# Recommendation tower on one core: each tile's pair products in one burst of matmuls, or in two with a turned chunk and a lookup between

## The reference

```python
e = jnp.stack([tbl_0[ids[:, 0]], ..., tbl_25[ids[:, 25]]], axis=1)      # 2048 x 26 x 128
combined = jnp.concatenate((dense[:, None, :], e), axis=1)              # 2048 x 27 x 128
interactions = jnp.einsum('bfd,bgd->bfg', combined, combined)           # 27 x 27 a sample
z = jnp.concatenate((dense, interactions[:, iu, ju]), axis=1)           # iu < ju: 351 pairs
h = jnp.concatenate([z, dense], axis=1)                                 # 2048 x 607
h = jnp.maximum(h @ W_top1 + b_top1, 0.0)                               # 512
h = jnp.maximum(h @ W_top2 + b_top2, 0.0)                               # 256
y = h @ W_top3                                                          # 1
```

## Time and profile before

| | |
|---|---|
| median of 3 runs | 529.42 us (525.82 to 533.13) |
| profiled execution | 532.02 us |
| its span, first to last instruction | 530.2 us |
| mean granted TensorE clock | 0.865 |
| busy: TensorE, VectorE, ScalarE, GpSimd | 74%, 50%, 30%, 50% |
| DMA | 35.02 MB, 66 GB/s in the mean |

### The profile page before, as it was taken

The page is one execution under the profiler, slowest core; times in us unless marked ns, Lnnn a source line. Parts: engine busy times, 40 slices in busy tenths (PEclk is TensorE's granted clock), DMA queues, the critical chain, the costliest instruction groups (busy, mean ns, idle before and its releaser), DMA issues.

```text
span 530.2 us, 14756 instructions
## 1 busy us (share of the span) xinstructions
PE 391.2 (74%) x6474; PEld 369.2 (70%) x6474; DVE 263.0 (50%) x761; ACT 159.9 (30%) x253; POOL 264.0 (50%) x282
## 2 busy tenths in 40 slices
PE   8459557857778788688878867786876687775877
PEld 7448546757668677588768856686866686774867
DVE  5267853554535564285463835284443743445123
ACT  3235322322313233132333323042322223323232
POOL 6757474462645626365564636375462635636000
PEclk9959687979878978788988987898977979789998
DMA  9933332131221312222222312222121321201000
GB/s 196 263 99 110 97 95 57 45 70 39 56 70 45 81 33 66 52 59 82 53 66 53 80 37 60 63 65 67 45 71 39 77 54 46 74 24 40 9 3 1
DMA packets 25333, 35.02 MB, mean 66 GB/s; under 512 B 8506, under 2 KB 19154, under 8 KB 25270
## 3 DMA queue, kind: packets, MB, share of 16 engines
q0 software_dynamic: 8768, 17.97, 13.4%
q1 hardware_dynamic: 14422, 15.96, 12.3%
q10 hardware_dynamic: 2080, 0.15, 0.4%
HBM read 34.05 MB, written 0.01 MB: 64 GB/s over the span
## 4 chain that ended last, share of the span: by engine, by line
PE 52%; another core or an unknown queue 17%; issue 15%; DVE 9%; ACT 6%; POOL 0%; POOLq 0%; DVEq 0%
PE side L608 18%; PE prod L641 10%; PE mlp L661 8%; DVE onehot L487 5%; PE side L619 4%; PE side L603 4%; DVE table L501 3%; PE mlp L663 3%; ACT feats L374 2%; ACT feats L381 2%; PE mlp L680 2%; PE mlp L672 1%; ACT diag L399 1%; PE side L650 1%
## 5 line engine op out<-in xcount | busy, mean ns | idle before, releaser
L354 POOL DMA_INDIRECT rows<-in_tbl,ids x274 | 263.2, 960 | 225.0 <-PE side L619 120.9
L487 DVE TENSOR_SCALAR onehot<-wanted,row_no 125x256 fp32r<-125x256 int32 (+1 forms) x564 | 171.7, 377 | 143.9 <-remote 59.7
L608 PE MATMUL side<-onehot,table_hi 125*128 125x256 f32 x566 | 164.0, 320 | 24.4 <-issue 16.2
L608 PE MATMUL side<-onehot,table_lo 125*128 125x256 f32 x566 | 157.0, 308 | 4.0 <-issue 3.9
L608 PEld LDWEIGHTS side<-onehot,table_hi 125*128 125x128 f32 x566 | 123.7, 219 | 30.3 <-issue 22.6
L608 PEld LDWEIGHTS side<-onehot,table_lo 125*128 125x128 f32 x566 | 123.6, 218 | 5.2 <-issue 5.2
L374 ACT ACTIVATE feats<-side 128x256 f32<-128x256 f32 x71 | 47.0, 662 | 176.6 <-remote 110.0
L381 ACT ACTIVATE feats<-side 128x512 f32<-128x512 f32 (+2 forms) x80 | 78.9, 1032 | 49.4 <-remote 46.3
L641 PE MATMUL prod<-feats 128*27 128x27 f32 (+1 forms) x4096 | 52.6, 211 | 50.0 <-issue 47.2
L641 PEld LDWEIGHTS prod<-feats 128*27 128x27 f32 (+1 forms) x4096 | 47.4, 124 | 54.1 <-issue 48.4
L619 PE MATMUL side<-ident,rows 128*128 128x128 f32 x274 | 48.9, 307 | 28.0 <-ACT feats L374 20.1
(11 more groups left out here) (53 smaller groups left out, 171.1 us busy)
## 6 DMA issues: line engine op xcount, KB each, us to landing
wanted<-in_small_ids SPq DMA_DIRECT2D x63, 128.0 KB
rows<-in_tbl,ids POOLq DMA_INDIRECT x274
feats<-in_tbl SPq DMA_DIRECT2D x7, 448.0 KB
dense<-in_dense_rows SPq DMA_DIRECT2D x16, 64.0 KB
w_sb<-in_w_pairs SPq DMA_DIRECT2D x1, 702.0 KB
table<-in_tbl SPq DMA_DIRECT2D x1, 560.0 KB
w_sb<-in_tbl SPq DMA_DIRECT2D x1, 560.0 KB
w_sb<-in_w SPq DMA_DIRECT2D x1, 512.0 KB
```

Of the source, the lines that this page charges most:

```text
L354: gp.indirect_dma_start(rows[:, q % SLOTS_OF_ROWS, f * D:(f + 1) * D], None, large_tables[g + f], bass.IndirectOffsetOnAxis(ap=ids[:, t, g ...
L487: made = nc.vector.tensor_scalar(onehot[v % 2][:, c - row_nos_at(h), :], wants, row_no[:, c:c + 1], None, ALU.is_equal)
L608: last = nc.tensor.matmul(look_bank(v)[:, 0:BS], part_of(part, k)[:, c * D:(c + 1) * D], onehot[v % 2][:, c, :], start=(c == 0 and part is ...
```

## The change

A tile's products come in two parts of 64 samples each (`PARTS`), part A at the head of segment 0 and part B at the head of segment 1. Between them stand segment 0's turned chunk and lookup. Each part writes one PSUM bank, of four (`PRODS`), where before a tile wrote a buffer of two banks, of two; ScalarE reads each part as it is done. The two relu stages of the layers go from VectorE to ScalarE, with one `ACTIVATE` in place of each `TENSOR_SCALAR`; the second layer's stands in segment 1 behind the lookup, the first layer's at the end of segment 3. ScalarE's copy of the result now stands before its copy of the pairs. VectorE makes the pair table in segment 1 instead of segment 0, behind that segment's one-hots. The last tile's products were in two parts already.

```diff
-BANK_GROUPS = 16
-PART_BANKS = 2
+PARTS = 2
+PART_GROUPS = GROUPS // PARTS
+PART_COLS = PART_GROUPS * SLOTS
...
+PRODS = 4
...
-        prod = [ctx.enter_context(nc.psum_tensor(f"prod{i}", [P, PART_BANKS * BANK], F32)) for i in range(2)]
+        prod = [ctx.enter_context(nc.psum_tensor(f"prod{i}", [P, BANK], F32)) for i in range(PRODS)]
...
+            def finish_first_layer(t):
+                act.wait_ge(l1_full, t + 1)
+                for n in range(N1):
+                    last = nc.scalar.activation(h1[:, n * P:(n + 1) * P], mlp[:, n * P:(n + 1) * P], ACT.Relu,
+                                                bias=b1_sb[:, n:n + 1])
+                last.then_inc(h1_ready, 1)
...
             for t in range(LAST):
                 for s in range(SEGS):
-                    if s == 0:
-                        read_products(t)
+                    if s < PARTS:
+                        read_products(t, s)
                     for k in TURNS_AT[s]:
                         empty_turn(t + 1, k)
                     if s == 1:
                         place_dense(t + 1)
                     for v in lookups_at(t, s):
                         empty_lookup(v)
+                    if s == 1 and t >= 1:
+                        finish_second_layer(t - 1)
                     if s == PAIRS_AT:
-                        copy_pairs(t)
                         if t >= 1:
                             copy_result(t - 1)
+                        copy_pairs(t)
+                    if s == 3:
+                        if t == 0:
+                            act.wait_ge(w_in, 5 * 16)
+                        finish_first_layer(t)
...
-                    if s == 0:
-                        if t == 1:
-                            dve.wait_ge(w_in, 5 * 16)
-                        if t >= 1:
-                            finish_first_layer(t - 1)
+                    if s == 1:
                         make_table(t)
...
-                    if s == 1 and t >= 1:
-                        finish_second_layer(t - 1)
...
             for t in range(LAST):
                 for s in range(SEGS):
-                    if s == 0:
-                        products(t)
+                    if s < PARTS:
+                        products(t, s)
                     for k in TURNS_AT[s]:
                         turn_rows(t + 1, k)
```

More of the change, by code:

```diff
@@ L260, in tail_bank @@
         def tail_bank(n):
[L261 removed]
+            return prod[n][:, 0:P]
         def spread_ids(k):
[L265 removed]
+            return prod[k // 2][0:CP, k % 2 * BS:(k % 2 + 1) * BS]
         def look_bank(v):
@@ L515, in finish @@
                 return nc.vector.tensor_scalar(out[:, n * P:(n + 1) * P], bank, bias[:, n:n + 1], 0.0, ALU.add, ALU.max)
[L517 to L525, removed]
-                    last = finish(h2, mlp[:, n * P:(n + 1) * P], b2_sb, n)
-                last.then_inc(h2_ready, 1)
             def clear_pads(i):
@@ L621, in turn_rows, with products @@
                 last.then_inc(turn_full, 1)
-            def products(t, r=0):
-                m = t + r
-                if t == 2:
-                    pe.wait_ge(pads_ready, 2 * FEAT_TILES)
+            def products(t, r):
+                m = PARTS * t + r
                 if r == 0:
+                    if t == 2:
+                        pe.wait_ge(pads_ready, 2 * FEAT_TILES)
                     pe.wait_ge(side_read, SIDE_OF["turn", NC * (t + 1) - 1] + 1)
@@ L630, in products @@
                     pe.wait_ge(dense_placed, t + 1)
-                if m >= 2:
-                    pe.wait_ge(prod_read, m - 1)
-                own = W if t < 2 else SLOTS
-                for k in range(parts_of(t)[r]):
-                    for g in range(BANK_GROUPS):
-                        for i in range(GS):
-                            n = ((r + k) * BANK_GROUPS + g) * GS + i
-                            at = t % FEAT_TILES * FT + n // 2 * TWO + n % 2 * W
-                            to = k * BANK + g * SLOTS
-                            last = nc.tensor.matmul(prod[m % 2][i * W:i * W + own, to:to + SLOTS],
-                                                    feats[:, at:at + own], feats[:, at:at + SLOTS],
-                                                    start=True, stop=True, tile_position=(0, i * W))
+                if m >= PRODS:
+                    pe.wait_ge(prod_read, m - PRODS + 1)
+                own = W if m < PRODS else SLOTS
+                for g in range(PART_GROUPS):
+                    for i in range(GS):
+                        n = (r * PART_GROUPS + g) * GS + i
+                        at = t % FEAT_TILES * FT + n // 2 * TWO + n % 2 * W
+                        last = nc.tensor.matmul(prod[m % PRODS][i * W:i * W + own, g * SLOTS:(g + 1) * SLOTS],
+                                                feats[:, at:at + own], feats[:, at:at + SLOTS],
+                                                start=True, stop=True, tile_position=(0, i * W))
                 last.then_inc(prod_full, 1)
```

26 lines of the change are left out of this document (15 added, 11 removed).

## The result

| | before | after |
|---|---|---|
| median, same chip | 529.5 us (525.82 to 533.13, 4 runs) | 505.22 us (501.41 to 508.68, 4 runs) |
| ratio | | **0.954**, 95% interval 0.9425 to 0.9655 |
| profiled execution, its span | 532.02, 530.2 us | 508.68, 506.9 us |
| mean granted TensorE clock | 0.865 | 0.882 |

A forecast was written before the change was run, and what follows sets the result against it. GpSimd's gathers were taken to set the beat, 31.0 us a tile; saving 1.0 us over 14 tiles (-14 us) took the profiled 532.0 to 518, the median 2.6 lower: 516 us, own range 508 to 524, 8 in 10 493 to 535.

The forecast's parts named there:

- GpSimd's gathers give the beat, T to T: From T, the first gather after a tile's first turned chunk, to the next T: 30.0 us against 31.0.
- Part A ahead of the first chunk, -3.5 us: Before the first turned chunk: half the matmuls save 1.6 us, the code stop 1.9; bounds 1.6 and 3.7.
- the drain: Between a tile's last gather and freely running products: 1.2 us while gathers drain.
- Part B, +2.1 us: Between first and second chunk: products crawl beside gathers, delaying gather round two by 2.1 us; upper bound +3.5.
- The rest of the tile "stays": After part B: rounds of 4, 4 and 5 gathers with two waits of 1.3 us, as in tile 5.
- ScalarE's relus, nothing: Relus of layers 1 and 2 moved to ScalarE cost nothing; bound +0.7 us a tile.
- Tile 0 unchanged: At the start: tile 0, like the tail, counted as unchanged; the saving covers 14 tiles only.
- The clock covered: Second lookup: another half-clock stretch after a second crawl, 1.4 us, covered by a late signal; without cover +0.5.
- four banks nothing: Four PSUM banks instead of two pairs remove no wait, as products never waited for a read: nothing.
- B is free: Rival, 20%: gathers don't hold part B, which is hidden in tiles like 4; 28.6 us a tile, 495 us.
- Stops stay: Rival, 17%: stops come from how products run, not the packet boundary, so each burst keeps one; 530 us.
- TensorE becomes late: Rival, 11%: crawls, half-clock stretches and late signals make TensorE late, third chunk ending after T+14.1; 543 us.

The follow-up runs named there:

- B behind the chunk: Changed kernel with part B right behind the first turned chunk, ahead of segment 0's lookups: 588.2 us, ratio 1.1023.
- B behind the second chunk: Changed kernel with part B behind the second turned chunk, in segment 1, instead of ahead of it: 573.35 us, ratio 1.0771.
- the third set: Changed kernel (374.11 us, 0.884) and three variants of it rerun beside the kernel before, unchanged, which took 423.58 us here and 538.43 in the first set.
- Split alone: Changed kernel with the relus of layers 1 and 2 back on VectorE: 521.49 us, ratio 0.975; rerun later at 375.39 us, ratio 0.8885.
- relus alone: Kernel before with the relus on ScalarE and the result's copy ahead of the pairs', products in one burst: 530.48 us, ratio 0.9915.
- B ahead of the chunk: Changed kernel with part B straight behind part A, ahead of the first turned chunk, four banks and ScalarE's relus kept: 534.82 us, ratio 0.9989.
- the kernel before once more: Kernel before, unchanged, run again for its trace on a third chip: 530.96 us beside 531.13 of its twin, ratio 1.006.
- the runs without gathers: Kernels before and after, each without the gathers of tiles 3 to 15 and the waits for them: 437.54 us (ratio 0.8215) and 386.25 us (0.7245).
- the second layer ahead of B: Changed kernel with the second layer of the tile before moved ahead of part B in even tiles: 375.49 us, ratio 0.8884.

## Why the prediction was right, step by step

**GpSimd's gathers give the beat, T to T.** Right in form and nearly in size: 29.7 for 30.0. The closeness is in part luck, as two terms below are each 0.7 us off and cancel. The sum itself is loose: its path (8.1 + 4.7 + ... + 1.1) adds up to 29.9 and not 29.8, and the parts, -3.5 and +2.1, make 1.4 us a tile, where it takes 1.0. By its parts it would have said about 510 (14 times 0.4 less).

**Part A ahead of the first chunk, -3.5 us.** Measured -2.77. The stops for code are gone (13 of 14 tiles before, none of 1.5 us or more that isn't a crawl after), and the halves cost 1.1 to 1.3 us unhindered. 0.7 us were oversized, inside the bounds of 1.6 and 3.7. What is missing is mostly the drain, for which the sum had 1.2 us: in nine of tiles 2 to 13 the long piece of A starts 1.7 to 1.9 us after the last gather has ended (tile 7: 266.83 and 268.67), and in tiles 5, 6 and 12 TensorE itself gets to A only 2.4 to 3.6 us after it.

**Part B, +2.1 us.** Measured +2.11 in the mean. B ends at T+6.4 to 6.8 (forecast 7.0), round two starts at T+7.3 to 8.1, 7.7 in the mean (forecast 8.1). The mean is of two kinds: even tiles, where B crawls, have round two 2.3 to 3.1 us later than before, odd ones 1.1 to 1.6. B behind the chunk and B behind the second chunk show the mechanism from both sides: the crawl lasts while gathers do.

**The rest of the tile "stays".** It lost 0.71 us of waits. Perhaps the wait before round two spaces the gathers, so that turned chunks and free places meet more evenly; no run separates it.

**ScalarE's relus, nothing.** On their own they gave 0.85% (interval 0.34 to 1.34%), some 4.6 us, possibly by a wait the prediction had not counted, the third layer's for VectorE. On top of the split no run resolves them: 0.954 and 0.975 come from different chips and their intervals nearly meet, and in the third set the two lie 0.3% apart. Split alone and relus alone multiply to 0.967; the rest to 0.954 isn't assigned.

**Tile 0 unchanged.** This step failed. It is also split, and its part A lets the first T come 1.9 us sooner (63.48 for 65.40); and the wait before round two breaks up a row of twelve gathers beside which TensorE had stood for 7.88 us. 7.9 us by tile 2, where the sum had 3 (its 14 tiles less the 11 from there on). That it is the split's doing fits the other traces: tile 2 has its T at 124.5 with the split alone, and at 129.3, 136.8 and 134.6 with the relus alone, with B ahead of the chunk and with the kernel before once more. Of the 9.3 us between the forecast's 14 and the 23.3 of the two spans, 4.9 are this term, 2.8 the tiles and 1.6 the end.

**The clock covered, four banks nothing.** Clock: 0.882 after 0.865, no loss. Banks: b ahead of the chunk has them and gains nothing, 0.9989.

**The rivals.** *B is free* (495) is wrong at this level, since B crawls, and right at the other: there both parts take 1.3 to 2.0 us from first to last start, but for one of tiles 0 to 14 (3.5). *Stops stay* (530) is excluded by the runs without gathers, by the packets that land at the stops, and by the order of B ahead of the chunk, which brings them back and lands at 534.82. *TensorE becomes late* (543) is what B right behind the chunk (588.2) and behind the second chunk (573.35) do: each passes the point that the prediction named, a third chunk later than T+14.1 (14.8 to 18.0 and 17.9 to 18.8 in tiles 2 to 13; 11.0 to 12.7 in the changed kernel).

**What stays open.** What makes TensorE crawl and signals come late. Gathers are needed (without them neither occurs), but they are not enough (in the third set they run back to back beside full-speed products). Something must be added that differs between sets of runs on one and the same chip, and no row of the profile names it. It isn't late code: in B of tile 2 handfuls go from 125.40 to 127.92, and packets of code were fetched at 122.2 and 129.5 only. Nor are transfers slower at the slower level: in the two traces of the changed kernel a packet of code takes 1.06 and 1.05 us in the mean, a packet of the gathers 0.12 and 0.13. One rival stands untested. Handfuls of five each 0.7 us are one matmul in some 0.15 us (an estimate from the rows of B right behind the chunk), close to the 0.12 us at which lookups start anyway. A limit on how fast instructions reach TensorE beside gathers would then hold up products and leave lookups alone. The experiment that was to tell this from other readings, the second layer ahead of B, ran at the level without a crawl.

## What to carry to other kernels

A long burst of small matmuls can outrun its own code. If a timeline shows "issue" stops that stand behind the same matmul in trace after trace, put other, slower work of the same engine in the middle: here 64 calls, a chunk and a lookup of 16 or more matmuls, then the other 64, and try it with the parts adjacent as well, since that shows at once whether the distance does it. Where an engine slows down beside another's transfers, place the moved work where the fewest transfers run beside it, behind something that would have to run in that time anyway. And take the kernel before along in every set of runs: here its own time moved by 21% between two sets, over four times the effect that was first measured.

## What the runs showed of the hardware

- Matmuls of the products beside gathers, in all traces with gathers but those of the third set: of a part that begins early in a round mostly 41 to 46 pass (B of even tiles), then one to six at a time with 0.7 us from handful to handful (some 1.4), until about 1 us after the last gather. Of a part that begins behind the first layer, late in the gathers, one to three pass (A of tile 7), and its long piece starts 1.7 to 1.9 us after the last gather. Other matmuls beside gathers aren't seen to do so: in tile 5 of the changed kernel 59 of lookups, layers and turns follow each other at 0.11 us in the mean from 218.50 on, while eight gathers run from 218.46.
- During a double round of gathers ScalarE, idle, goes on 5.6 us after TensorE's lookup has ended (224.2 and 229.85 in tile 5). That the semaphore comes late is a reading; the profile shows "remote" as the cause.
- In the third set, the same programs without either: 374.11 us for 505.22, 423.58 for 530 to 538; why is open.
- Stops for code: 1.9 to 2.8 us without any gather near, behind pieces of 158 to 243 matmuls, and TensorE goes on 1.2 to 1.6 us after the packet has landed. With 128 matmuls at a time and a chunk and a lookup between, they are gone but for single ones (1.0 us without gathers, 1.72 in the third set).
